# A decoder layer whose attention normalises the softmax: the division moved from GpSimd into the split to high and low halves, in the unit's own step

## The reference, cut to what matters

```python
x = x + attention(layernorm(x))        # causal, 32 query heads, 8 key/value heads of 128
x = x + fake_quant(layernorm(x)) @ fake_quant(ctx)
x = x + low_rank_experts(layernorm(x)) # 64 experts, top 16
# attention, for x of 2 batches x 512 tokens x 1024:
scores = q @ k.T / sqrt(128)           # masked above the diagonal
attn   = softmax(scores)               # exp(s - max) / sum of the row
out    = (attn @ v) @ Wo.T
```

## Time and profile before

| | |
|---|---|
| median of three runs | 1134.34 us |
| profiled execution, whole | 1134.8 us |
| its span (first to last instruction) | 1133.0 us |
| mean granted PE clock | 0.991 |
| PE / DVE / ACT / POOL busy | 95% / 80% / 47% / 36% of the span |
| attention, from the first scores to the last Wo chunk | about 136 to 975 us |

### The profile page before, as it was taken

The page is one execution under the profiler, slowest core; times in us unless marked ns, Lnnn a source line. Parts: engine busy times, 40 slices in busy tenths (PEclk is TensorE's granted clock), DMA queues, the critical chain, the costliest instruction groups (busy, mean ns, idle before and its releaser), DMA issues.

```text
span 1133.0 us, 19870 instructions
## 1 busy us (share of the span) xinstructions
PE 1077.2 (95%) x6361; PEld 580.2 (51%) x6368; DVE 907.1 (80%) x1868; ACT 536.7 (47%) x1094; POOL 411.0 (36%) x423
## 2 busy tenths in 40 slices
PE   4999988999999999999999999999999999799997
PEld 3876544455545554555555455545554544345553
DVE  6789588978787878788888878787978897888853
ACT  4656366544444545454445545454545462343421
POOL 2049655534343435334343534343534242000000
PEclk8999999999999999999999999999999999999999
DMA  7026147544454445445545544444545578000001
GB/s 300 1 82 236 75 93 155 139 109 118 125 132 105 100 122 147 111 121 129 114 102 135 136 111 104 120 120 111 128 123 114 124 180 267 1 1 38 35 23 56
DMA packets 200865, 128.66 MB, mean 114 GB/s; under 512 B 171376, under 2 KB 173552, under 8 KB 199920
## 3 DMA queue, kind: packets, MB, share of 16 engines
q1 hardware_dynamic: 200816, 128.03, 43.4%
HBM read 68.23 MB, written 17.83 MB: 76 GB/s over the span
## 4 chain that ended last, share of the span: by engine, by line
PE 78%; DVE 10%; DMA 3%; ACT 3%; issue 3%; SPq 1%; POOL 0%; DVEq 0%; ACTq 0%; POOLq 0%
PE ps L1535 73%; DMA k_t<-kv_parts 3%; PE ps L1785 3%; DVE prob L1297 2%; ACT prob L968 1%; DVE wo_sb L1091 1%; DVE h_b L1091 1%; DVE prob_s L1091 1%; SPq L526 1%; DVE stats L1099 1%; PE ps L1801 1%; PE ps L1853 1%; DVE prob_t L1091 1%; DMA o_t<-in_wdown 1%; PE ps L1549 0%
## 5 line engine op out<-in xcount | busy, mean ns | idle before, releaser
L705 POOL TENSOR_SCALAR prob<-prob,row_inv 128x128 f32<-128x128 f32 (+3 forms) x256 | 203.4, 813 | 450.5 <-DVE row_inv L1268 450.5
L1535 PE MATMUL ps<-wo_sb,o_t 128*128 128x512 f16 x1536 | 351.2, 380 | 3.7 <-DVE x_sb L1279 3.6
L1535 PE MATMUL ps<-h_b,wq_sb 128*128 128x512 f16 x1524 | 340.9, 380 | 0.0
L968 ACT ACTIVATE prob<-prob,neg_max 128x128 f32<-128x128 f32 (+3 forms) x256 | 140.6, 550 | 234.1 <-DVE neg_max L1303 234.1
L1535 PEld LDWEIGHTS ps<-h_b,wq_sb 128*128 128x128 f16 x1524 | 148.3, 98 | 177.4 <-issue 0.3
L1535 PEld LDWEIGHTS ps<-wo_sb,o_t 128*128 128x128 f16 x1536 | 147.2, 98 | 172.4 <-DVE x_sb L1279 6.9
L1279 DVE SCALAR_TENSOR_TENSOR x_sb<-ps,x_sb 128x512 f32<-128x512 f32 x256 | 174.2, 686 | 54.9 <-PE ps L1535 53.9
L1535 PE MATMUL ps<-k_t,q_t 128*128 128x512 f16 (+3 forms) x768 | 115.3, 301 | 10.6 <-DMA k_t<-kv_parts 9.3
L1535 PE MATMUL ps<-prob_t,v_sb 128*128 128x128 f16 (+2 forms) x960 | 118.0, 277 | 6.3 <-DMA prob_t<-prob_s 6.3
L1297 DVE CUSTOM_DVE_ANT_0 prob<-ps,mask 128x512 f32<-128x512 f32 (+3 forms) x256 | 110.3, 485 | 2.3 <-issue 1.6
L1255 DVE SCALAR_TENSOR_TENSOR q_tmp<-ps,q_tmp 128x512 f32<-128x512 f32 x105 | 72.1, 687 | 40.4 <-PE ps L1535 38.4
(11 more groups left out here) (141 smaller groups left out, 1172.9 us busy)
## 6 DMA issues: line engine op xcount, KB each, us to landing
wq_in<-in_wq SPq DMA_DIRECT2D x64, 256.0 KB, 3.4
wo_in<-in_wo SPq DMA_DIRECT2D x32, 512.0 KB, 3.9
side_in<-in_ctx SPq DMA_DIRECT2D x16, 512.0 KB, 4.4
kv_parts<-wo_sb SPq DMA_DIRECT2D x7, 1024.0 KB, 5.3
x_sb<-in_x SPq DMA_DIRECT2D x8, 512.0 KB, 9.3
ctx_quantised<-side_out SPq DMA_DIRECT2D x16, 256.0 KB, 2.9
h_b<-ctx_quantised SPq DMA_DIRECT2D x2, 2048.0 KB, 11.2
out<-x_sb SPq DMA_DIRECT2D x8, 512.0 KB, 2.6
```

What stands on the lines that cost most here:

```text
L705: ins = nc.gpsimd.tensor_scalar(at, at, row_inv[:, u % 2, q:q + 1], S_P, ALU.mult, ALU.mult)
L968: ins = nc.scalar.activation(at, at, ACT.Exp, bias=neg_max[:, n % 2, q:q + 1], scale=SOFTMAX, accum_out=row_sum[:, n % 2, q:q + 1])
L1535: ins = nc.tensor.matmul(out_, lhs(i), rhs(j), start=start and n == 0, stop=stop and n == 3 * len(pairs) - 1)
```

## The change

ACT's and DVE's `p_split` move into the unit's own step, behind its o_split (ACT) and the add of chunk 1 (DVE). The POOL normalisation is gone. DVE makes `row_inv` with a second small instruction that multiplies by S_P, behind a wait for the reciprocals. The high half is now written by four ACT copies with `row_inv` as scale, one for each piece, since each piece has its own column of reciprocals; the low half by four DVE instructions that multiply `prob` by `row_inv` and subtract the high half.

```diff
@@ POOL, group
                     m = 2 * g + u // PAIR_UNITS
-
-                    pool.wait_ge(inv_done, UNITS * g + u + 1)
-                    pool.sem_inc(pool_passed)
-                    for q in range(QT):
-                        at = prob[:, u % 2, S_AT[q]:S_AT[q] + (q + 1) * P]
-                        ins = nc.gpsimd.tensor_scalar(at, at, row_inv[:, u % 2, q:q + 1], S_P, ALU.mult, ALU.mult)
-                    ins.then_inc(prob_normed, 1)
@@ ACT, p_split
-                act.wait_ge(prob_normed, UNITS * g + n + 1)
+                act.wait_ge(inv_done, UNITS * g + n + 1)
...
-                split_hi(prob_s[:, 0, :], prob[:, n % 2, :], p_hi, 1.0)
+                for q in range(QT):
+                    at = slice(S_AT[q], S_AT[q] + (q + 1) * P)
+                    ins = nc.scalar.activation(prob_s[:, 0, at], prob[:, n % 2, at], ACT.Copy, scale=row_inv[:, n % 2, q:q + 1])
+                ins.then_inc(p_hi, 1)
@@ ACT, group
-                    if not (first and u == 0):
-                        p_split(g, u - 1)
                     exponentials(g, u)
                     if not (first and u < LAG):
                         o_split(g, u - LAG)
+                    p_split(g, u)
@@ ACT, behind the groups
-            p_split(KV_HEADS - 1, UNITS - 1)
@@ DVE, inverses and p_split
-                nc.vector.reciprocal(row_inv[:, n % 2, :], row_sum[:, n % 2, :]).then_inc(inv_done, 1)
+                nc.vector.reciprocal(row_inv[:, n % 2, :], row_sum[:, n % 2, :]).then_inc(inverted, 1)
+                dve.wait_ge(inverted, UNITS * g + n + 1)
+                nc.vector.tensor_scalar(row_inv[:, n % 2, :], row_inv[:, n % 2, :], S_P, None, ALU.mult).then_inc(inv_done, 1)
...
-                split_lo(prob_s[:, 1, :], prob[:, n % 2, :], prob_s[:, 0, :], p_lo, 1.0)
+                for q in range(QT):
+                    at = slice(S_AT[q], S_AT[q] + (q + 1) * P)
+                    ins = nc.vector.scalar_tensor_tensor(prob_s[:, 1, at], prob[:, n % 2, at], row_inv[:, n % 2, q:q + 1],
+                                                         prob_s[:, 0, at], ALU.mult, ALU.subtract)
+                ins.then_inc(p_lo, 1)
@@ DVE, last_outputs
-                    if i == 2:
-                        p_split(g, UNITS - 1)
```

More of the change, by code:

```diff
@@ L307, in decoder_layer @@
         pow_done = sem("pow_done")
-        prob_normed = sem("prob_normed")
+        inverted = sem("inverted")
         var_done = sem("var_done")
```

## The result

The changed kernel takes 1218.88 us (median of 4 runs, 1218.14 to 1222.35) against 1134.01 us before (4 runs, 1131.15 to 1134.78): ratio 1.0758, 95% interval 1.0736 to 1.0781. It is 84.9 us slower where 55.4 were forecast, and 7 us above the top of the range. The direction and the mechanism came as forecast; the size was a third too small. The profiled execution's span is 1216.4 us (1133.0 before).

A forecast was written before the change was run, and what follows sets the result against it. PE bound the kernel before; DVE would bind after. First group 100.2, six groups of 110.0 and a last of 86.3 made 846.5 us, 53.3 more; with 2.1 behind them 55.4, so 1190 us. Own range 1178 to 1200, full range 1160 to 1212.

The forecast's parts named there:

- What bounds the kernel now: Kernel before: PE is the bound; its waits for k_t (9.3 us) and prob_t (6.3) could give back at most 15.6.
- The cover of the exponentials: DVE's step: the old split filled the 2.45 us from neg_max to the reciprocals; moved, only a 0.60 us add fits.
- The pieces and the second wait: DVE's step: its split starts 2.40 us after the reciprocals, behind ACT's four copies; DVE's four pieces take 1.84 us.
- head: First part of each DVE step, from the maxima through the split: 8.53 us until DVE gets to the rest.
- The rival of the cheaper pieces: DVE's pieces and ACT's copies cost less, a step is 0.34 us shorter: 1169 us; chance 0.12.
- POOL's ctx_sum adds: Two POOL adds per group, in steps 3 and 7, slow DVE's query splits: 3.0 us a group, half in the first.
- The rival of no loss beside POOL: POOL's ctx_sum adds cost DVE nothing, since POOL works half as long as before: 1170 us; chance 0.13.
- DVE's group of 107.0 us: DVE's work in a group of eight steps: 107.0 us, above PE's 104.1, so DVE becomes the bound.
- Together 38.8 us: Rest of DVE's steps in a group: blocks, combines, adds, queries, side operations and Wo splits, 38.8 us.
- the tail behind the last maxima: After the last unit's maxima, the add that PE's last chunks wait for begins later: 2.1 us more.
- The clock: Rival: PE's clock falls behind waits for DVE, 1.7 us lost in each of eight groups: 1204 us; chance 0.11.
- The faster rival: With a step's head below 7.8 us PE stays the bound and its 15.6 us of waits vanish: 1119 us; chance 0.05.

The follow-up runs named there:

- e3: Changed kernel with DVE's loop over the six middle groups written out as straight code; 1205.68 us, ratio 1.0629 to the kernel before.
- e10: Changed kernel with DVE's loop written out and POOL's ctx_sum add on 8 of 1024 columns; 1189.18 us, ratio 1.0494 to the kernel before.
- e11: As e10, with POOL's four sums of wq blocks also on 8 of 512 columns behind the first; 1176.46 us, ratio 1.0380.
- e2: Changed kernel with one ACT copy and one DVE piece of 1280 columns, the division by the row sum left out; 1164.80 us, ratio 1.0266.
- e4: Changed kernel with POOL's ctx_sum add on 8 of 1024 columns, loop still rolled; 1209.87 us, ratio 1.0665 to the kernel before.
- e5: Kernel before with only the splits moved into the unit's own step, old arithmetic with POOL's normalisation kept; 1279.32 us, ratio 1.1288.

## Why the prediction fell short

*What bounds the kernel now: right.* PE bound it, and of the 15.6 us that it might give back the 9.3 for k_t did come back once their cause was edited. The 6.3 for prob_t no run took away in the old order.

*The cover of the exponentials: right.* 2.45 us forecast from `neg_max` to the reciprocals, 2.43 measured between the same two places (568.15 to 570.58); moving the split back regained 82 us.

*The pieces and the second wait: right.* Reciprocals to split 2.40 forecast, 2.44 measured; four pieces 1.84 and 1.86; head 8.53 and 8.59. The rival of the cheaper pieces fell on its own durations.

*POOL's ctx_sum adds: right in a full group, short in the first.* 3.0 us a group were taken; from e3 to e10 the middle groups fall by 2.75 (111.65 to 108.9). In the first group I took half of it, but both adds cost there too: its steps 3 and 7 fell by 1.8 and 1.4 us with the add made small. In the second group it gave 1.6 and in the last one nothing. Over the whole kernel it is 16.5 us for the 19.5 in the sum. The rival of no loss beside POOL (1170) fell with it.

*DVE's group of 107.0 us: right as a sum of DVE's own work, wrong as the length of a group.* With the loop written out and POOL's instructions small it is 107.19; the changed kernel's is 114.3, for the 110.0 of the sum. This is the step that failed: "Together 38.8 us. With 8 x 8.53 = 68.2 a group takes DVE 107.0 us", and upon it 3.0 for ctx_sum alone. Two terms are missing in it.
1. The jump. I counted instructions by duration and not by number. The change takes DVE's body over the size up to which the jump back is free: 13.2 us for the loop with its five jumps, by the kernel with the loop written out, of which 11.0 are idle time at the jumps. That "issue" stood in the profile of before, 1.6 us ahead of the maxima, and I passed it over.
2. `neg_max` behind POOL's wq sums: 12.7 us by the run that makes the sums small, 1.7 in a full group (two places of 0.85). I had looked for POOL only beside the query splits, where the earlier trace rows show it; the sums of wq blocks move against DVE's step as everything does when the step grows, and one of them now falls on the one small instruction that ACT waits for. The prediction had "or twice that, if POOL, freed of its wait, meets more of DVE's splits" as a bound, and 2.75 and 1.7 us for the 3.0 is about half way there.

The account of the missing 28.9 us (1218.9 less 1190): 13.2 for the jumps, 12.7 for the wq sums, less 3.0 by which the ctx_sum term was too large, leaves 6.0. These are in e11 too, where neither jump nor POOL counts (1176.5 for 1190 less 19.5): 1.6 in the tail behind the last maxima (206.0 for 202.3, 2.1 forecast), 1.3 in the second group, and 0.2 to 0.8 in each of the others; the last half microsecond is rounding and time outside the span. What they are is open, and so is the exact share of each term: the runs differ from one another by a microsecond or two.

*The range.* It was put together from rivals that all changed the same terms. None was for a cost that is no instruction, and the upper end allowed for POOL or the clock alone, not for the two things that came together.

*The clock.* The condition of this rival came in part, its price didn't. PE waits 61 times for DVE, up to 4.5 us. From the first scores to the last Wo chunk the granted clock stands at the lower of its two levels in six stretches, 24 us in all (three and 14 us in the kernel before), for instance behind a wait of 2.02 us that ends at 475.64. The stretch, its length, PE's busy time and, third from the end, the granted clock:

```profile
476.50:479.80 3.30, 3.30 (x11) 1.35 (x10) 3.30 (x7) 1.25 (x3) 0.65 (x1) 0.50 0.61 119
```

The group that it lies in takes 114.3 us, and so do its neighbour without one (114.2) and the rest. In the groups PE's slower work is hidden by DVE's. Whether it costs something in the tail no run shows.

*The faster rival* fell at its condition, a head below 7.8 us. And the condition was not enough: in e2 the head is 7.50 us (556.37 to 563.87), and the time is 1164.8, not 1119, since the 7.8 left out the same jump and POOL's other instructions.

## What to carry to other kernels

A piece of work that fills a wait of its engine costs little there, and the wait stays when the work is moved: before moving a step, write down the chain that stands in the wait it filled. An engine's busy share (DVE's is 77% here, and it sets the pace) doesn't tell whether it is the bound; add up one step of it with the gaps. A change that adds instructions to an engine with a rolled loop should be checked at the jump, for here it cost 2 to 3 us an iteration though each instruction is short, and a gain just ahead of such a jump can vanish into it. And test the cheap edit that the wait list names first: one line of SyncE's order gave 9.3 us, the whole change of arithmetic none.

## What the runs showed of the hardware

- A jump back on DVE is free up to some size of body (0.22 us idle) and costs 2.1 to 2.9 us above it, with 32 instructions between the two. The profile calls it "issue". The wait is not a fixed price: with shorter work ahead of it, it grew to 3.2 to 3.5 (e2) and 3.5 to 4.9 us (e4). It ends 1.7 to 2.1 us after a transfer of code has ended, in 30 of 30 jumps; what sets the start of that transfer is open.
- A DVE instruction of 128x4, 0.17 us by itself, took 1.02 us beside a POOL instruction of 128x512.
- POOL's multiplications by a pointer took 532 ns on average with DVE waiting and 813 ns beside a working DVE: 692 against 1736 ns for 512 columns, 371 in both for 128.
- A DVE split of 128x512 with two SBUF sources (`b_out`), 0.68 us by itself, took 1.76 us beside a POOL instruction of 128x512 (e2, e5).
- A copy on ACT with a pointer as its scale takes what an exponential of the same shape takes: 402 ns for 128 columns (0.40 in the earlier trace rows), 492 for 256 (0.49), 706 for 512.
